# The spot comparison's three parts move ahead of the low bits and the plain one-hot in each batch of five VectorE steps

## The reference, cut to what matters

```python
hw = jnp.einsum('ni,rio->rno', h, weight)            # 8 relations + 1
msg = hw[rel, src] + bias[rel]
agg = jax.ops.segment_max(msg, dst, num_segments=n)
...
out = hw[-1] + agg + bias[-1]
```

## Time and profile before

| | |
|---|---|
| median of 3 runs | 2650.6 us (2649.99 to 2651.94) |
| profiled execution | 2652.58 us |
| its span | 2650.7 us |
| GpSimd busy / TensorE / VectorE / ScalarE | 1490.7 / 1977.3 / 1328.0 / 670.7 us |

### The profile page before, as it was taken

The page is one execution under the profiler, slowest core; times in us unless marked ns, Lnnn a source line. Parts: engine busy times, 40 slices in busy tenths (PEclk is TensorE's granted clock), DMA queues, the critical chain, the costliest instruction groups (busy, mean ns, idle before and its releaser), DMA issues. The chain is left out here.

```text
span 2650.7 us, 33489 instructions
## 1 busy us (share of the span) xinstructions
PE 1977.3 (75%) x11712; PEld 1095.3 (41%) x11712; DVE 1328.0 (50%) x3186; ACT 670.7 (25%) x1332; POOL 1490.7 (56%) x1528
## 2 busy tenths in 40 slices
PE   6744545555554545436899999998999999799996
PEld 3411111111121111124555555554555555467775
DVE  6466666666666666654322222221323332357775
ACT  4244445445454444424200000000000000100000
POOL 4277777777777777760156666663576657400000
PEclk8855655656565655568999999999999999899998
DMA  5545555555555555564354454465444444610000
GB/s 177 184 130 159 168 166 160 172 157 162 157 162 156 162 165 168 156 203 166 129 172 160 148 171 150 150 144 144 163 149 161 131 161 147 104 40 1 1 6 21
DMA packets 183331, 370.18 MB, mean 140 GB/s; under 512 B 38760, under 2 KB 119254, under 8 KB 174838
## 3 DMA queue, kind: packets, MB, share of 16 engines
q1 hardware_dynamic: 129208, 263.74, 28.1%
q0 software_dynamic: 48704, 101.21, 16.4%
q10 hardware_dynamic: 5246, 3.03, 0.4%
HBM read 232.54 MB, written 135.28 MB: 139 GB/s over the span
## 5 line engine op out<-in xcount | busy, mean ns | idle before, releaser
L925 POOL DMA_INDIRECT arena<-table_rel,key_rel x784 | 789.0, 1006 | 278.0 <-issue 233.6
L1053 PE MATMUL ps_out<-arena 128*128 128x400 f16 x1024 | 380.4, 509 | 438.2 <-DVE arena L959 396.6
L1097 ACT ACTIVATE arena<-ps_out 128x800 fp8e4<-128x800 f32 x512 | 400.2, 834 | 437.1 <-PE ps_out L1053 436.9
L1575 POOL DMA_INDIRECT arena<-table_cut,src_at x324 | 312.6, 965 | 277.2 <-DMA table_cut<-Z 111.7
L943 DVE SCALAR_TENSOR_TENSOR arena<-arena,keep_max 128x128 f32<-128x128 f32 x784 | 275.3, 351 | 328.5 <-DMA arena<-table_rel,key_rel 318.6
L1575 POOL DMA_INDIRECT arena<-table_next,src_at x324 | 314.9, 972 | 186.6 <-issue 91.8
L1053 PEld LDWEIGHTS ps_out<-arena 128*128 128x128 f16 x1024 | 85.3, 117 | 656.4 <-DVE arena L959 409.6
L1853 PE MATMUL ps_out<-arena,Z 128*128 128x512 fp8e4 x1600 | 352.3, 380 | 0.0
L1853 PE MATMUL ps_out<-arena,cut 128*128 128x512 fp8e4 x1600 | 350.2, 379 | 0.0
L959 DVE TENSOR_TENSOR arena<-iota,arena 128x1072 f16<-128x1072 f16 (+1 forms) x384 | 271.5, 707 | 0.0
L1269 PE MATMUL ps_out<-arena,cut 128*128 128x384 fp8e4 (+1 forms) x1500 | 207.9, 300 | 45.3 <-PEq L116 43.5
(11 more groups left out here) (312 smaller groups left out, 1993.8 us busy)
## 6 DMA issues: line engine op xcount, KB each, us to landing
arena<-adjacency SPq DMA_DIRECT2D x64, 1600.0 KB, 7.0
adjacency<-arena SPq DMA_DIRECT2D x160, 320.0 KB
running_rows<-arena SPq DMA_DIRECT2D x392, 128.0 KB
arena<-adjacency_plain SPq DMA_DIRECT2D x50, 400.0 KB, 9.4
table_rel<-arena SPq DMA_DIRECT2D x25, 512.0 KB, 2.9
arena<-table_rel,key_rel POOLq DMA_INDIRECT x784, 2.9
adjacency_plain<-adj SPq DMA_DIRECT2D x50, 128.0 KB, 2.5
arena<-table_cut,src_at POOLq DMA_INDIRECT x324
```

The lines of the kernel that those rows point to most:

```text
L925: e.indirect_dma_start(message(t), None, table, bass.IndirectOffsetOnAxis(key[:, t:t + 1], 0)).then_inc(s_msg[t % both], 16)
L1053: last = e.matmul(g.ps_out[:, u % 2, x * 512:x * 512 + KW], g.hot_low[:, q % 2, k, :, x], g.hot_spot[:, b % 2, k, :, x], start=True, stop= ...
L1097: e.activation(g.half[h % 2].rearrange("p (a w x) -> p a w x", a=NT, x=R * WIN)[:, :, at:at + 2, :], g.ps_out[:, u % 2, 0:1024].rearrange( ...
L1575: e.indirect_dma_start(g.picked[:, w % 2 * BLOCKS + k, :, :].rearrange("p a f -> p (a f)"), None, tables[y], bass.IndirectOffsetOnAxis(g.s ...
```

## The change

Within a full batch VectorE used to make the low bits at the first step, the plain one-hot at the second, and the three spot parts at the third to fifth. Now the three spot parts come at the first three steps, the low bits at the fourth and the plain one-hot at the fifth. No instruction is added or removed, and the other engines' programs are the same.

```diff
             for i in range(TRIPLES):
                 for x in range(2):
                     t, q, b = i * SLOTS + x * 5, 3 * i + x, 2 * i + x
-                    step(t)
+                    for k in range(3):
+                        step(t + k)
+                        spot(b, k)
+                    step(t + 3)
                     low(q)
-                    step(t + 1)
+                    step(t + 4)
                     flat(q)
-                    for k in range(3):
-                        step(t + 2 + k)
-                        spot(b, k)
                 step(i * SLOTS + 10)
                 low(3 * i + 2)
                 step(i * SLOTS + 11)
```

## The result

The changed kernel takes 2634.49 us (median of 5 runs, 2630.13 to 2639.29) against 2650.62: a ratio of 0.9938, 95% interval 0.9923 to 0.9953. The direction and the wait were right, the size was not.

What follows compares the result with a forecast made beforehand. GpSimd's gathers were taken to bound the pass. A 7 us gain, between 5.3 (wait alone) and 12.9, gave 2652.6 - 7 = 2645.6 profiled; the median, 2.0 lower, 2643.6 us, range 2637 to 2651.

Steps and rivals of the forecast that it cites:

- What bounds the pass: GpSimd's 784 gathers set the pace of the gather pass; 46.6 us lost inside its instructions over their 0.947 us.
- The straddle: GpSimd loses time only when a VectorE instruction straddles an issue's start by more than 0.13 us; 0.39 us in one example.
- The wait: VectorE's low bits waiting for TensorE's counts of a full batch, 28 waits and 16.9 us, go whole.
- Low end of the gain: the wait alone: Issues 12i+3 and 12i+4 take 0.144 us less where step 0's low bits didn't wait; times 37, 5.3 us.
- The third reason given for not expecting more: In the gather pass, a vanished delay leaves GpSimd earlier against VectorE, making the next straddle a little likelier; no size given.
- I take 7 us, in the lower third: Gain chosen for the gather pass between 5.3 and 12.9 us, giving 2643.6 us.
- The circle is only turned: Long and short steps keep their cyclic order, two steps earlier, so part of issues +7 and +0's loss returns; unsized.
- The first ground: Step 0's low bits that did not wait still lost 0.140 us at issue +3, many through late landings; these stay.
- the five items of the high end: Issues 12i+3, +4, +9, +7, +0 each take the loss their new kind of work has elsewhere; sum 12.9 us.
- the straddles only move: Rival, chance 0.31: nine long comparisons stay in the pass, so gain 0 to 5 us, 2646 to 2651 us.
- steps 1 and 6 would be dear: Rival, chance 0.07: late landings make new long comparisons there straddle as often as step 0's late low bits; 2657 us.
- the wait would stay: Rival: TensorE starts its batch later, so low bits of steps 10 and 15 wait; about 2650 us, chance within 0.31.

Runs made afterwards that it cites:

- the second execution: The changed kernel, unaltered, measured again beside three variants on one chip: 2634.2 us against 2646.4 for the kernel before, ratio 0.9947.

## Why the prediction was wrong

**What bounds the pass: right.** The change of the pass (17.2 us) is the change of GpSimd's busy time (17.2), and nothing else moved as much.

**The straddle: right.** Its rule (VectorE's end less 0.13 us, if VectorE was there first) gives 0.53 us in the changed kernel, and over both traces it gives 94% of the issues within 0.03 us. The inference of the Trainium skill (SBUF — State Buffer, Who interferes with whom), by which a tensor_tensor takes only the read interface and would leave descriptor making alone, does not hold for these issues: the 256 that met a comparison lost 30.6 us.

**The wait: right, and its price right in the sum alone.** "Low end of the gain: the wait alone", 5.3 us, measured 6.6 with the wait alone taken away. But the 5.3 were worked out for issues 12i+3 and 12i+4, and there 12.6 came back; that 7.1 were lost again elsewhere makes the two agree, and that is luck. The third reason given for not expecting more, that a delay which falls away makes other straddles likelier, is what the 7.1 show in the old order.

**The step that failed is "I take 7 us, in the lower third"**, with its ground, "The circle is only turned, so a part of what issues +7 and +0 lose will come back two steps earlier". Nothing came back there: issues 12i+5 went from 64.45 to 64.60 us and 12i+10 from 62.09 to 61.93, summed as above. The first ground, that late landings at step 0 stay, holds for 2.7 us of this trace at issues +3, and for none in the second execution, where they take 63.50 us in all, 0.045 lost each (over 0.947). Of the five items of the high end, measured against predicted: +3 6.0 of 8.7 us; +4 1.9 of 0.3; +9 -0.1 of -3.3; +7 5.1 of 5.6; +0 1.9 of 1.7. Together 14.8 against 12.9. The two new long steps, 1 and 6, were priced at the average, 0.054 us each; they cost (62.47/64 - 0.944) = 0.032 and 0.006. And the other 400 issues gained 3.6 where nothing was put, while issues +2 lost 1.1. The high end, which took each step at its own price, was the better sum, though that its items add up so well is in part luck: some are off by 3 us in opposite directions. I argued it away with a symmetry that the kernel doesn't have: what stands at a step is turned, but not how late its fold begins. The mean time from an issue's start to its fold's start, from the two traces, is longest for step 3 (3.25 us before, 3.15 after) and shortest for step 6 (2.68 and 2.66), whatever VectorE does there.

**The rivals.** That the straddles only move is refuted for the change as a whole (the loss fell by a third, from 46.6 to 31.7 us). That steps 1 and 6 would be dear came out the opposite way. That the wait would stay did not happen.

**Not settled.** Why some steps are dear and others cheap was not tried. The mean lag of the folds fits step 6 (2.66 us after the change, cheap) and step 4 (3.06, dear), but it does not part step 1 (2.88, cheap) from step 8 (2.96), and why the folds of some steps come later is open. The share of chance is large too: the same program's pass took 1009.5 and 1005.2 us in two executions, on issues 12i+3 alone 3.3 us apart, so 12 to 16 us is as closely as the gain is known.

## What to carry to other kernels

When an engine's instructions have a constant minimum and a long tail, sum the tail by position in the loop before pricing a reorder. Then take each position at its own price, also where the order after looks like the order before turned round: what is fixed to the step (here how late its fold begins) doesn't turn. Such a price is no constant either: when one short step moved from 9 to 8, other issues took back what one gave.

Where an indirect DMA's descriptors set the pace, a wait on VectorE that lengthens no queue can still cost, because it decides what runs when the next issue begins. Removing it gave 6 to 7 us, half of its local price; the place of the short instructions gave the rest, 11 us where the two were compared in one series.

Cutting a long instruction in two makes the whole longer. Here what the gap between the halves gave back, the longer pair took again.

Time a change of half a per cent on more than one chip. Here the same pair of kernels gave 0.9938 and 0.9947 in two series and 1.0021 on another chip.

## What was not expected of the hardware

- Two halves of a comparison, 0.42 us each and overlapping by 0.09, mostly hold an issue one half at a time (42 of 49). In the three traces with halves, all 68 issues that were held on to the second half's end met a pair that VectorE began while it was behind. Where it had waited for a landing before the pair, none was held on so, and 53 were held to the first half's end. What makes the difference is not shown.
- Who is first is decided within some 0.02 us of the issue's start. In the traces before and after, 37 comparisons began 0.00 to 0.10 us after it, behind a running fold, and none held the issue beyond the fold's own end less 0.13 us; the one at 243.90, in the halves, did. One that begins later runs inside the issue at its usual length (412.90, 0.68 us).
- A fold holds an issue by the same rule as a comparison (81 issues, 2.4 us before).
- On two chips the pass had episodes about every 100 us in which TensorE, ScalarE or VectorE stood between instructions, VectorE for 35 us at a time, and the kernel took 300 us longer. In a pass without TensorE's products they appeared on the other engines.
